# Two chained cross-attentions: the first body in another order, its first weight products block by block, and prediction rows 2 and 3 ahead in the body before last

## What is computed

```python
# layer 0: softmax over axis 1 (the rows of x), scale = 512 ** -0.5
q = emb @ Wq + bq;  k = latent @ Wk + bk;  v = latent @ Wv + bv
w = softmax(einsum('bte,bme->btm', q, k) * scale, axis=1)
x = einsum('btm,bme->bte', w, v) + emb
x = (x - mean) * rsqrt(var + EPS) * gamma + beta
# layer 1: softmax over axis -1
Q = query @ Wq + bq;  K = key @ Wk + bk;  V = key @ Wv + bv
attended = softmax(Q @ K.T * scale, axis=-1) @ V
out = query + attended @ Wo + bo
```

## Time and profile before

| | |
|---|---|
| median of three timed runs | 684.29 us (684.04 to 684.96) |
| the profiled execution, its own time | 682.88 us |
| its span, first to last instruction | 680.8 us |
| busy: PE, DVE, ACT, POOL | 98%, 76%, 62%, 72% of the span |
| mean granted clock of PE | 0.997 |

### The profile page before, as it was taken

One profiled execution on the slowest core, in us unless ns is written; L12 is line 12 of the kernel. 1 busy time (PEld: TensorE's weight loads), 2 busy tenths in 40 slices (PEclk: granted clock), 3 DMA queues, 4 the chain that ended last, 5 costly groups with the idle time before them and its releaser, 6 DMA issues.

```text
span 680.8 us, 12411 instructions
## 1 busy us (share of the span) xinstructions
PE 667.1 (98%) x4047; PEld 589.4 (87%) x4047; DVE 520.4 (76%) x1227; ACT 424.6 (62%) x1037; POOL 490.3 (72%) x394
## 2 busy tenths in 40 slices
PE   8988999999999999999999999999999999999987
PEld 6975888989898898889889888988989898898976
DVE  4889687877868787786878778796877779687765
ACT  2765666576666747666575766656566665666542
POOL 0566968769596877959687795968778695866762
PEclk9998999999999999999999999999999999999999
DMA  9902005050220505032050503104040401302003
GB/s 296 317 6 77 32 2 171 1 170 0 73 96 0 169 0 170 0 94 76 0 169 0 170 0 121 48 10 159 0 170 0 142 28 40 129 0 78 1 1 124
DMA packets 34657, 53.47 MB, mean 79 GB/s; under 512 B 4560, under 2 KB 12752, under 8 KB 34640
## 3 DMA queue, kind: packets, MB, share of 16 engines
q1 hardware_dynamic: 34640, 53.26, 23.7%
HBM read 36.44 MB, written 16.81 MB: 78 GB/s over the span
## 4 chain that ended last, share of the span: by engine, by line
PE 89%; DVE 5%; POOL 2%; ACT 1%; DMA 1%; issue 1%; SPq 0%; DVEq 0%; POOLq 0%
PE bank L418 77%; PE bank L425 12%; DVE n L898 1%; DMA bk_b<-in_L_xattn_bk_dram 1%; POOL n L1215 1%; DVE stats L1054 1%; POOL wq_sb L1221 1%; DVE x_even L1049 0%; DVE rb L981 0%; DVE xT_lo L874 0%; DVE n L1065 0%; POOL rstd L1227 0%; ACT bank L747 0%; ACT n L715 0%; SPq L322 0%
## 5 line engine op out<-in xcount | busy, mean ns | idle before, releaser
L1234 POOL TENSOR_TENSOR prod<-n,u_b 128x512 f32<-128x512 f32 x64 | 81.5, 1297 | 44.7 <-DVE n L1065 39.3
L872 DVE SCALAR_TENSOR_TENSOR y_lo<-bank,terms,y_hi 128x512 fp32r<-128x512 f32 x64 | 48.0, 749 | 62.8 <-ACT y_hi L665 62.8
L1273 POOL TENSOR_TENSOR r<-r,beta_b 128x512 f32<-128x512 f32 x60 | 76.0, 1298 | 0.0
L1266 POOL TENSOR_TENSOR r<-n,gamma_b 128x512 f32<-128x512 f32 x60 | 75.7, 1299 | 0.0
L665 ACT ACTIVATE y_hi<-bank,terms 128x512 fp32r<-128x512 f32 x64 | 43.9, 686 | 39.9 <-PE bank L418 39.9
L1227 POOL TENSOR_TENSOR rstd<-var_eps,minus_half 128x2 f32<-128x2 f32 x32 | 22.4, 699 | 63.5 <-DVE var_eps L1061 63.4
L667 ACT ACTIVATE pc_hi<-bank 128x512 fp32r<-128x512 f32 x32 | 19.2, 598 | 68.2 <-PE bank L418 68.2
L1038 DVE SCALAR_TENSOR_TENSOR r<-bank,rinv,r 128x512 f32<-128x512 f32 x60 | 44.8, 747 | 11.2 <-PE bank L418 11.2
L418 PE MATMUL bank<-wv_hi,wc_hi 128*128 128x512 f32 x128 | 51.6, 403 | 1.8 <-issue 1.8
L747 ACT ACTIVATE bank<-e,neg 128x256 f32<-128x256 f32 x64 | 29.9, 468 | 35.1 <-DVE neg L1000 35.1
L418 PE MATMUL bank<-xT_hi,wqk_hi 128*128 128x512 f32 x128 | 51.2, 400 | 0.0
(11 more groups left out here) (201 smaller groups left out, 2355.0 us busy)
## 6 DMA issues: line engine op xcount, KB each, us to landing
out_dram<-r SPq DMA_DIRECT2D x15, 1024.0 KB, 5.4
x_even<-in_x_dram SPq DMA_DIRECT2D x8, 1024.0 KB, 7.2
ctxn<-in_ctx_dram SPq DMA_DIRECT2D x16, 512.0 KB, 3.7
x_odd<-in_x_dram SPq DMA_DIRECT2D x8, 1024.0 KB, 7.0
rb<-r_rows SPq DMA_DIRECT2D x15, 256.0 KB, 3.8
wq_sb<-in_L_xattn_Wq_dram SPq DMA_DIRECT2D x4, 256.0 KB, 3.4
wk_sb<-in_L_xattn_Wk_dram SPq DMA_DIRECT2D x2, 512.0 KB, 6.8
wv_sb<-in_L_xattn_Wv_dram SPq DMA_DIRECT2D x2, 512.0 KB, 9.2
```

Of the source, the lines that this page charges most:

```text
L872: i = dve.scalar_tensor_tensor(dst, src, bias, high.bitcast(F32), ALU.add, ALU.subtract)
L1234: pool.tensor_tensor(prod[j % 2][:], N[:, j, :], u_b[1][:], ALU.mult).then_inc(prod_ready, 1)
L1266: pool.tensor_tensor(r[:, j, :], N[:, j, :], gamma_b[:], ALU.mult).then_inc(scaled_ready, 1)
L1273: pool.tensor_tensor(r[:, j, :], r[:, j, :], beta_b[:], ALU.add).then_inc(resid_ready, 1)
```

## The change

- SyncE loads Wk0 first, in two blocks of rows, then the four blocks of Wq0.
- PE transposes Wk0 first, runs two further warm-up products, and then transposes each block of Wq0 into a bank of its own; the product of one block follows while the next one is loaded. The copies of these transposes on ScalarE and VectorE go by blocks of rows too.
- The dots for `u0` move on VectorE from before `wqk0`'s low parts to behind the context's; the spread of `u0` moves on PE behind `y`, and `first_row_terms0` behind y's low parts.
- PE transposes Wv1 together with Wq1 and Wk1, ahead of the scores; `rb` is spread between the two halves of the scores; betaq is spread behind `wc`; `u1` between the two halves of `wvo`.
- ScalarE does `bv_wo` and then all four `beta_terms` behind the weights of the softmax; wqk1 is rounded in two halves between other steps.
- VectorE takes wqk1's low parts in two halves inside `norm_and_output`, adds betaq behind wc's low halves, and takes wvo's first low half before the last two normalisations.
- POOL adds up `bv_wo` right behind the sum of w's low parts; the products for the next pair's row terms are spread over its other steps, and rstd of the second half comes before the products with `u1`.
- The banks follow: `u0` 5, `q1` 3, `wvT1` 2 and 3, `wqk1` 6 and 7, `u1` 1, `bo1` 7.
- In the body before last, PE does `pr` 2 and 3 ahead of both `pc`, and VectorE adds block 3 and normalises all four blocks before pc's second low half.

```diff
-PREP0 = tiles("wqT0", 4) + tiles("wkT0", 2) + tiles("wqk0", 2) + tiles("u0", 1)
-PREP1A = tiles("wqT1", 4) + tiles("wkT1", 2)
-PREP1B = tiles("wvT1", 2) + tiles("wqk1", 2) + tiles("q1", 1)
-PREP1C = [("u1", 0), ("wvo", 0), ("wvo", 1), ("bo1", 0)]
-
-PREP_BANKS = (7, 0, 1, 2, 3, 4, 5, 6, 7) + (0, 1, 2, 3, 4, 5) + (6, 7, 2, 3, 6) + (3, 6, 7, 4)
+PREP0 = tiles("wqT0", 4) + tiles("wkT0", 2) + tiles("wqk0", 2)
+PREP1A = tiles("wqT1", 4) + tiles("wkT1", 2) + tiles("wvT1", 2)
+PREP1B = tiles("wqk1", 2)
+PREP1C = [("wvo", 0), ("u1", 0), ("wvo", 1), ("bo1", 0)]
+
+PREP_BANKS = (7, 0, 1, 2, 3, 4, 5, 6) + (0, 1, 2, 3, 4, 5) + (2, 3, 6, 7) + (3, 1, 6, 7)
...
-    bank["rb", 0] = 7
+    bank["u0", 0], bank["rb", 0], bank["q1", 0] = 5, 7, 3
...
+            for c in range(KC):
+                sp.dma_start(wk0_sb[:, c, :], wk0[c * P:(c + 1) * P, :]).then_inc(wk0_loaded[c], 16)
             for k in range(KD):
                 sp.dma_start(wq0_sb[:, k, :], wq0[k * P:(k + 1) * P, :]).then_inc(wq0_loaded[k], 16)
-            sp.dma_start(wk0_sb[:], wk0.rearrange("(k p) e -> p k e", p=P)).then_inc(loaded["wk0"], 16)
...
+                def wq_block(k):
+                    pe.wait_ge(wq0_loaded[k], 16)
+                    transposes(it, "wqT0", k, [wq0_sb[:, k, e * P:(e + 1) * P] for e in range(KD)])
+
+                def product_of_block(k):
+                    wait_emptied(pe, it, "wqT0", k)
+                    weight_product(it, 0, wqT0, wkT0, k)
+
                 pe.wait_ge(ident_ready, 2)
-                for k in range(KD):
-                    pe.wait_ge(wq0_loaded[k], 16)
+                for c in range(KC):
+                    pe.wait_ge(wk0_loaded[c], 16)
                     for e in range(KD):
-                        mm = pe.transpose(at(("wqT0", e))[:, k * P:(k + 1) * P], wq0_sb[:, k, e * P:(e + 1) * P],
-                                          ident[:])
-                        if k == KD - 1:
-                            end(mm, "wqT0", e)
-                transpose_kv(it, "wkT0", wk0_sb, loaded["wk0"])
-                weight_products(it, 0, wqT0, wkT0)
+                        g, h = divmod(e, 2)
+                        mm = pe.transpose(at(("wkT0", g))[:, (h * KC + c) * P:(h * KC + c + 1) * P],
+                                          wk0_sb[:, c, e * P:(e + 1) * P], ident[:])
+                        if c == KC - 1 and h == 1:
+                            end(mm, "wkT0", g)
+                warm_up(BANK["wqk0", 1], 2)
+                wq_block(0)
+                wq_block(1)
+                for g in range(2):
+                    wait_emptied(pe, it, "wkT0", g)
+                product_of_block(0)
+                wq_block(2)
+                product_of_block(1)
+                wq_block(3)
+                product_of_block(2)
+                product_of_block(3)
...
+                transpose_kv(it, "wvT1", wv1_sb, loaded["wv1"])
...
                 pe.wait_ge(betaq_ready, KD)
                 spread(it, "q1", betaq)
+
             def prepare1c(it):
-
-                pe.wait_ge(u_ready, 2)
-                spread(it, "u1", terms[1])
                 for g in range(2):
                     wait_emptied(pe, it, "wvT1", g)
                 pe.wait_ge(loaded["wo1"], 16)
                 for c in range(KC):
+                    if c == 1:
+                        pe.wait_ge(u_ready, 2)
+                        spread(it, "u1", terms[1])
                     dst = begin(it, "wvo", c)
                     end(product(dst[:], [(wvT1[:, h, c * P:(c + 1) * P], wo1_sb[:, h, :])
                                          for h in range(KD)]), "wvo", c)
...
...
                 if begin_it:
+                    spread_u0(it)
                     prepare1a(it)
                 if it.back:
                     transpose_n(it)
                 if it.last:
                     apply(it, "late", 1, "pc", PC, WVO)
                 if begin_it:
+                    scores0(it, (0,))
                     spread_first_r0(it)
-                if it.front:
+                    scores0(it, (1,))
+                elif it.front:
                     scores0(it)
                 if begin_it:
                     prepare1b(it)
...
                     weigh0(it, 0)
                     row_sums(it)
                     weigh0(it, 1)
+                if begin_it:
+                    spread_betaq(it)
                 if it.back:
                     scores1(it)
                 if it.last:
...
                 if it.back:
                     transpose_probs(it, 0)
                     transpose_probs(it, 1)
+                if it.before_last:
+                    apply(it, "pr", 2, "wc", WC, WV0)
+                    apply(it, "pr", 3, "wc", WC, WV0)
                 for b in range(2):
-                    if it.front:
+                    if it.front and not it.before_last:
                         apply(it, "pr", 2 + b, "wc", WC, WV0)
                     if it.back:
...
             def finish_first(it):
 
-                for b in range(2):
-                    round_bank(it, "wc", b, halves(WC[0], b))
+                round_bank(it, "wc", 0, halves(WC[0], 0))
+                prepare1b(it, (0, 1))
+                round_bank(it, "wc", 1, halves(WC[0], 1))
                 for j in range(J):
                     bias_of_rows(it, j)
+                prepare1b(it, (2, 3))
+                round_bank(it, "wvo", 0, WVO[0][:, 0, :])
+                copy_bank(it, "u1", 0, u_b[1][:])
                 next_row_terms0(it)
-                copy_bank(it, "u1", 0, u_b[1][:])
-                bv_wo(it)
-                round_bank(it, "wvo", 0, WVO[0][:, 0, :])
                 row_terms(it, (0, 1), 0)
...
...
                 if it.last:
                     row_terms(it, range(J), 1)
                     shifted_row_terms(it)
-                if begin_it:
-                    beta_terms(it, (0, 1))
                 if it.front:
                     exponentials0(it)
                     weights0(it)
                 if begin_it:
-                    beta_terms(it, (2, 3))
-                    prepare1b(it)
+                    bv_wo(it, range(KD))
+                    beta_terms(it, range(KD))
                     act.wait_ge(rows_in_or_stored, 16 * ROWS)
...
+                for k in (1, 3):
+                    wait_filled(dve, it, "wqT0", k)
+                    dve.tensor_copy(wqT0[:, :, k * P:(k + 1) * P],
+                                    at(("wqT0", k))[:].rearrange("p (e d) -> p e d", e=KD))\
+                       .then_inc(emptied[BANK["wqT0", k]], 1)
...
                 wk_bq(0, wk0_sb, bq0_b, bk0_b, N)
+                low_wqk(it, 0, lambda k: SCALE)
+
+            def row_terms0(it):
                 for k in range(KD):
                     dve.wait_ge(wq0_loaded[k], 16)
-                wq_bk(0, wq0_sb, bk0_b)
+                wq_bk(0, wq0_sb, bk0_b, range(KD))
                 dots_done()
                 dve.tensor_scalar(terms[0][:, :KD], dots[0][:, :KD], SCALE, None, ALU.mult).then_inc(u_ready, 1)
-                low_wqk(it, 0, lambda k: SCALE)
...
                 if it.front:
                     add(0)
                     statistics(0)
+                    if not it.back:
+                        prepare1b(it, 0)
                     add(1)
...
+                if not it.back:
+                    prepare1b(it, 1)
+                if it.before_last:
+                    add(3)
+                    statistics(3)
+                    dve.wait_ge(stats_ready, it.times(J, J))
+                    aggregate(1)
...
                     normalise(1)
-                    add(3)
-                    statistics(3)
-                if it.before_last:
-
-                    dve.wait_ge(stats_ready, it.times(J, J))
-                    aggregate(1)
-                if it.back:
-                    cut_pc(1)
                 if it.before_last:
                     normalise(2)
                     normalise(3)
+                elif it.front:
+                    add(3)
+                    statistics(3)
+                if it.back:
+                    cut_pc(1)
...
+                if not it.back:
+                    low_wvo(it, 0)
...
                     if begin_it:
-                        first_row_terms0()
+                        row_terms0(it)
                     for c in range(KC):
                         low(it, "y", c, Y[1][:, c, :], Y[0][:, c, :], bias=ccol[0][:, c:c + 1], per=KC)
+                    if begin_it:
+                        first_row_terms0()
                 if begin_it:
                     prepare1a(it)
                     cut_v0(it)
...
                     normalise0(it)
                 if begin_it:
                     row_terms1(it)
-                    prepare1b(it)
-                    add_betaq(it)
                     low(it, "wc", 0, halves(WC[1], 0), halves(WC[0], 0), per=2)
...
+                if begin_it:
+                    add_betaq(it)
...
-                    low_wvo(it, 0)
...
```

(15 more changed lines are left out.)

113 lines of the change are left out of this document (60 added, 53 removed).

## The result

The changed kernel takes 686.49 us (median of 7 runs, 686.32 to 686.70) against 682.90 for the kernel before (7 runs, 682.34 to 684.96; the three of them shown at the start are the upper ones). The ratio is 1.0038 [1.0025, 1.0051], while the two medians lie 0.53% apart, since the runs of the kernel before spread over 2.6 us: slower, by a quarter to half a per cent. The profiled execution takes 686.4 us with a span of 684.4, where the earlier trace rows belongs to a span of 680.8.

What follows compares the result with a forecast made beforehand. TensorE, busy for 98% of the span, bounds the kernel, so its holes and clock decide. +2.7 (Y) +1.5 (clock) -0.8 (end) = +3.4 on 682.88 gives 686.3, median 687.7; range 681.6 to 690.4.

Steps and rivals of the forecast that it cites:

- The start: First body: second layer's products start at 32.75, now 32.36, held by Wv1's landing at 28.5; nothing gained at P.
- P: Start of the first `pr` in the first body: 45.38 before, forecast 47.65, +2.3.
- The softmax: Body 0: maxima due about 31.9, before 30.39; exponentials at 33.0 against 32.28, +0.7, bounds +0.4 and +2.2.
- Dots and P: Layer 1's dots on VectorE: first at 41.7, all four lasting 5.0 us, giving P 47.65, +2.3.
- Rivals 1 and 2: Layer 1's dots unhindered beside POOL: 682.4, faster, chance 0.22; the same with the clock lowered once: 683.9, no change, 0.18.
- Rival 3: VectorE instructions meeting POOL each cost a whole POOL product: dots 6.1, P 49.05, Y 71.05, 689.8; chance 0.09.
- Y: Start of body 1's projection on PE: 66.22 before, forecast 68.95, +2.7.
- From P to Y: First `pr` to body 1's projection: 21.3 us, now 20.84, ends 20.3 and 22.0; xT's rounding late, not `bo1`.
- Clock: PE idle 3.3 us ahead of Y, lowering its clock: 1.5 us charged, bounds 0 and 1.6.
- rival 4: As forecast, but PE's hole ahead of Y doesn't lower the clock: +1.9, 686.2; chance 0.11.
- Last bodies: VectorE's way to n's transposes loses pc's second low half and a wait for POOL's root: -0.8, bounds -0.5 and -1.0.
- Sum and median: +2.7 (Y) +1.5 (clock) -0.8 (end) = +3.4 on 682.88: 686.3; median 687.7, from 1.41 between median and profiled execution.

Runs made afterwards that it cites:

- the last bodies alone: Kernel before with only the change's last-bodies part (`pr` 2 and 3 ahead of both `pc`, four normalisations earlier): 682.05 us, ratio 0.9981.
- wc's low half first: Kernel before with changed last bodies and `bv_wo` in gaps, plus wc's low halves and row sums ahead of wqk's low parts and betaq's addition: 680.80 us.

## Why the prediction came out as it did

**The start.** Wv1 was called a load that the change doesn't move, landing at 28.5. It was issued at 20.51 instead of 21.63 (why, no run shows), and landed 6.4 us later, at 26.9. The second layer's products therefore began at 31.14 and not at 32.75. That this buys nothing at P held: it only made the hole ahead of P 5.67 us, where the text came to some 3.6.

**The softmax.** The maxima came at 31.84 where 31.9 was forecast, but not because `rb` was copied late (its copy ended at 30.51): `cut_v0` stood ahead of them for 3.42 us, beside POOL's cut of the context. That mechanism stood in the text as an upper bound of +2.2, but with everything earlier ahead of it the exponentials began only 0.36 us later than before (32.64), below the forecast's +0.7 and its lower bound of +0.4. That the maxima's number was right is luck: two errors, TensorE earlier and VectorE later, met in it.

**Dots and P.** The first dot came at 41.30 (forecast 41.7), released by ScalarE: 2.45 us later by `bv_wo`, 1.23 by the two sums and 0.38 by what lies ahead of them, where the sum had 2.54, 1.22 and 0.7. The dots took 5.7 us for the 5.0 kept from before (41.30 to 47.0), inside the bounds of 2.5 and 6.1; the first of them now met POOL for all of its length (1.70 for 1.09). P 47.86 against 47.65: the 0.4 too much and the 0.7 too little nearly cancel. The dots' start and their company were then shown apart, by exchanging two lines and by thinning POOL. Rivals 1 and 2, dots unhindered, fell. Rival 3's 6.1 us for the dots was nearer to the 5.7 than my 5.0, but its Y of 71.05 didn't come.

**From P to Y.** 21.37 us against 21.3. The second pair of normalisations began at P + 13.4 (forecast 13.3); from there to Y it took 7.9, between the two ends given (7.0 and 8.7). The collisions on that way cost 2.97 us (2.89 for two normalisations that alone take 1.00, and 1.76 for a dot of 0.68), no less than the 2.95 of the kernel before: what `bv_wo`'s sums gave up there, `xprod` 3 and the products with u1 took. One step was wrong in kind: the low clock after P was to hide behind VectorE's work altogether, but add(0) waited 1.02 us for TensorE and add(1) 0.34. With the clock up add(0) waited as long for POOL, so only add(1)'s part was the clock's; keeping it up gave 0.49 us at Y.

**Clock.** The hole ahead of Y was 2.32 us instead of 3.3, as the fall after P lasted 5.2 us and cost TensorE 2.6, not the 1.5 in its sum (16.5 + 2.6 = 19.1 from P to the hole, forecast 18.0). The text expected the fall because 3.3 is more than the 2.82 that lowered the clock before. The hole was shorter than that, and the clock fell nonetheless, at a price of 1.6 us instead of 1.5: the charge was right, its reason was not. Length alone doesn't decide it, as holes of 1.79 and 1.80 us in one and the same first body show (the last bodies alone, above). That it fell a whole us after TensorE had resumed was not in the text (rival 4 would have been taken for true by anyone looking at the first us alone).

**Last bodies.** -0.9 against -0.8, confirmed alone (-0.8). The hole of about 1 us that the text expected there came as 0.64 ahead of `out` 0 and 0.17 ahead of n's transposes.

**Sum and median.** Y +3.0, clock +1.6, end -0.9 give +3.7 for a forecast of +3.4; the span grew by 3.6. On the profiled execution the text said 686.3, and it was 686.4. The mechanism was right; the term of the sum that was mis-sized is the last: 1.41 us were added because the three timed runs of the kernel before stood so far above its profiled execution. That gap doesn't belong to every kernel. The changed kernel's seven runs lie within 0.4 us of its profiled execution; the kernel before's 96 runs beside the experiments go from 681.97 to 686.99 in step with their mean granted clock (below). The forecast's 687.7 is therefore 1.2 too high, and its loss of 0.50% lies at the upper end of the ratio's interval, 0.25 to 0.51%.

The Trainium skill ("SBUF — State Buffer", Who interferes with whom) states that VectorE and GpSimd lock a shared pair of ports for a whole instruction, and that a VectorE instruction with at most one SBUF input, outside the modes that use both ports, doesn't contend. The traces agree: the 128x4 term took 2.23 us beside a sum of 1024 columns (0.16 without it), and wqk's low parts, which read one bank and one tile, took 1.65 for four wholly beside the same sums (45.09 to 46.74, in the kernel with wc's low half first) and 1.66 without them (the kernel before).
